# Mamba scan with B and C rows spread by DMA, half of its drives made by ScalarE, and sixteen experts loaded after it

## The reference

```python
xin, z = split(layernorm(x) @ in_proj.T)
xc  = silu(causal_conv8(xin))
dt, B, C = split(xc @ x_proj.T)              # 8, 16 and 16 columns
delta = softplus(dt @ dt_proj.T + bias)
h_t = h_(t-1) * exp(delta_t * A[:, n]) + delta_t * B_t[n] * xc_t      # for each channel and state n
y_t = sum over n of h_t * C_t[n]
out = ((y + xc * D) * silu(z)) @ out_proj.T  # then residual, norm and a 128-512-128 ReLU network
```

## Time and profile before

| | |
|---|---|
| median of 3 runs | 788.13 us (787.86 to 789.38) |
| span of the profiled execution | 791.8 us, from its first to its last instruction |
| the profiled execution's own time | not listed apart from its span; the span is 3.7 us above the median of the runs |
| busy: PE, DVE, ACT, POOL | 642.2, 529.6, 405.3, 414.8 us |
| DMA | 84.43 MB |

### The profile page before, as it was taken

How to read it: one execution, slowest core, us unless ns; L and a number is a source line. 1 busy time by engine, 2 the same in 40 slices (tenths; PEclk the granted TensorE clock), 3 DMA queues, 4 the chain that set the end, 5 groups by cost and what they waited for, 6 DMA issues and landing times.

```text
span 791.8 us, 17837 instructions
## 1 busy us (share of the span) xinstructions
PE 642.2 (81%) x4583; PEld 434.2 (55%) x4583; DVE 529.6 (67%) x1518; ACT 405.3 (51%) x880; POOL 414.8 (52%) x488
## 2 busy tenths in 40 slices
PE   4974888888865599999287799999888648999890
PEld 2311333324653499999143355555456517999890
DVE  6779999996565266555378889899645633665444
ACT  2645777772321165665075567677644303566550
POOL 5203999985667255454277534444444672545450
PEclk9965999999995799999699599999999867999995
DMA  7979999922011122221618311211002112222215
GB/s 205 321 254 256 251 247 249 249 58 80 8 34 47 53 81 70 72 72 41 185 36 287 128 51 49 59 49 35 4 0 98 34 53 58 78 71 67 67 42 166
DMA packets 88312, 84.43 MB, mean 107 GB/s; under 512 B 12897, under 2 KB 77401, under 8 KB 87977
## 3 DMA queue, kind: packets, MB, share of 16 engines
q1 hardware_dynamic: 82600, 71.89, 33.9%
q0 software_dynamic: 5632, 11.58, 4.5%
HBM read 37.98 MB, written 45.46 MB: 105 GB/s over the span
## 4 chain that ended last, share of the span: by engine, by line
PE 33%; DVE 7%; issue 5%; DMA 2%; SPq 2%; ACT 2%; POOL 1%; ACTq 0%; DVEq 0%; POOLq 0%
PE bank L643 7%; PE bank L652 6%; PE bank L2017 5%; PE bank L1948 3%; PE bank L1951 2%; DVE t_peak L1768 2%; PE bank L2127 2%; PE bank L1993 2%; PE bank L2118 1%; DVE X L249 1%; PE bank L636 1%; SPq L1427 1%; DMA work<-results 1%; PE bank L2044 1%; DVE t_tabs L1848 0%
## 5 line engine op out<-in xcount | busy, mean ns | idle before, releaser
L806 POOL TENSOR_TENSOR UN<-work 128x512 f32<-128x512 f32 x64 | 81.7, 1289 | 55.4 <-DVE work L1034 54.7
L1768 DVE TENSOR_REDUCE t_peak<-bank 128x1 f32<-128x512 f32 (+2 forms) x192 | 104.0, 592 | 9.5 <-PE bank L1951 7.4
L445 ACT ACTIVATE t_v_tiles<-bank,t_e_b1all 128x128 f32<-128x128 f32 x224 | 64.0, 368 | 63.5 <-PE bank L643 58.8
L445 ACT ACTIVATE m_dx_tiles<-bank,m_e_b1all 128x128 f32<-128x128 f32 x224 | 64.0, 369 | 60.0 <-PE bank L643 57.8
L410 POOL DMA_INDIRECT results<-t_A,t_e_to_row x56 | 53.8, 961 | 67.1 <-DVE t_A L559 33.0
L410 POOL DMA_INDIRECT results<-m_XC,m_e_to_row x56 | 53.8, 961 | 63.7 <-issue 33.9
L1181 PE MATMUL bank<-UN,ident 128*128 128x512 f32 x128 | 71.0, 637 | 14.2 <-POOL UN L806 13.6
L1034 DVE TENSOR_TENSOR_SCAN work<-bank,work 128x512 f32<-128x512 f32 x64 | 76.6, 1216 | 8.3 <-POOL UN L806 7.0
L549 DVE COPY UN<-w1all 128x512 f32 x112 | 48.2, 430 | 40.5 <-PE bank L643 28.4
L652 PE MATMUL bank<-w2all,t_v_tiles 128*128 x448 | 60.6, 279 | 2.7 <-ACT t_v_tiles L445 2.0
L643 PE MATMUL bank<-t_A,UN 128*128 128x128 f32 x448 | 61.0, 280 | 0.0
(11 more groups left out here) (323 smaller groups left out, 1441.8 us busy)
## 6 DMA issues: line engine op xcount, KB each, us to landing
xrows<-m_nothing SPq DMA_DIRECT2D x25, 1032.0 KB, 17.9
w1all<-in_e_w SPq DMA_DIRECT2D x6, 1024.0 KB, 12.2
work<-results SPq DMA_DIRECT2D x16, 256.0 KB, 4.5
m_dx_tiles<-xrows SPq DMA_DIRECT2D x56, 64.5 KB
t_v_tiles<-xrows SPq DMA_DIRECT2D x56, 64.5 KB
t_tabs<-stacks SPq DMA_DIRECT2D x32, 96.0 KB, 2.2
work<-stacks SPq DMA_DIRECT2D x32, 96.0 KB, 2.1
m_tabs<-in_e_b SPq DMA_DIRECT2D x1, 1536.0 KB
```

Source lines behind the costliest of these rows:

```text
L445: ins = act.activation(e.hid[:, mp, f * P:f * P + P], core.tiles(2 + mp)[:, f, :], ACT.Gelu, bias=row(e.b1all, x)[:, f:f + 1])
L806: g.tensor_tensor(hc[:, k % 4, :], h[:, k % 2, :], c_sb[:, k % 2, :], ALU.mult).then_inc(hc_ready, 1)
L1768: v.tensor_reduce(peak[p][:, a, ss[0]:ss[-1] + 1, qt], bank[:, f, 0:len(ss) * w].rearrange("p (j n) -> p j n", n=w), AX_X, ALU.max).then_i ...
```

## The change

1. **B and C rows.** `split`, `pick`, `spread_b`, `spread_c` and ACT's copies of C are gone. `select` is one f32 matmul for all 40 columns. ACT copies its result (`keep_sel`), and SP writes the 32 rows of B and C to HBM and reads each row back over all partitions, 256 KB a transfer: 64 for C into eight buffers and 32 for B into four. The buffers lie where the last 16 experts' weights go.
2. **Drives.** The pattern `DAGADADAGADADAGA` says who makes the drive of each of 16 steps. In 8 steps (A) ACT scales time-major tiles of `DX` by a column of B in four instructions of 128 columns, and PE turns them into a PSUM bank with four transposes. In 5 steps (D) DVE multiplies the B row, now in SBUF, by `DX`; in 3 (G) POOL does.
3. **Buffers.** `h` has four buffers instead of two. Decays have six: three in PSUM, for D and G steps, and three in SBUF, for A steps. So a scan still has one input in PSUM and one in SBUF.
4. **Step sizes.** Only batch 0's part of softplus on DVE is done ahead of the scan. Of batches 1 to 3 the four DVE instructions (of 512 columns) follow steps 2, 4, 6 and 8 of the batch before. On PE six matmuls on the identity stand ahead of the first transposes of `DX`.
5. **Experts.** Eight experts are loaded at the start and 16 after the scan. The 25.8 MB of zeros are gone: once the rows are counted, SP and ACT each write 12 blocks of 64.5 KB behind the last row of 12 experts, ahead of SP's reads and of ACT's gates, in both mixtures.

```diff
-REGION = NB * T
+REGION = NB * T + P
+KINDS = "DAGADADAGADADAGA"
+LATE_EXPERTS = 8
...
+    def clear_ends(self, eng, experts):
+        e, core = self, self.core
+        eng.wait_ge(e.end_row_ready, 1)
+        for x in experts:
+            r = eng.value_load(e.end_row[0:1, x:x + 1], min_val=0, max_val=XROWS - P)
+            eng.dma_start(core.xrows[bass.ds(r, P), :], core.nothing[:]).then_inc(core.zeroed, 16)
...
     def sync(self, sp):
         e, core = self, self.core
+        e.clear_ends(sp, range(0, NE, 2))
+        sp.wait_ge(core.zeroed, 16 + 16 * NE * e.layer)
         sp.wait_ge(core.sent, 16 * TOPK * NT * e.layer)
...
     def scalar(self, act):
         e, core = self, self.core
+        e.clear_ends(act, range(1, NE, 2))
         act.wait_ge(e.gdiff_ready, 1)
...
+            def keep_rows(b):
+                sp.wait_ge(sel_copied, b + 1)
+                sp.dma_start(bc_rows[b], sel[b % 2][0:2 * NS, :]).then_inc(rows_kept, 16)
+                sp.wait_ge(rows_kept, 16 * b + 16)
+            def stream(k):
+                b, n, i = k // NS, k % NS, before(B_STEPS, k)
+                if kind(k) != "A":
+                    if i >= 4:
+                        sp.wait_ge(h_ready, LEAD + B_STEPS[i - 4] + 1)
+                    sp.dma_start(b_sb[:, i % 4, :], bc_rows[b, n].partition_broadcast(P)).then_inc(core.back_in[i % 4], 16)
+                if k >= AHEAD:
+                    sp.wait_ge(hc_ready, LEAD + k - AHEAD + 1)
+                sp.dma_start(c_sb[:, k % AHEAD, :], bc_rows[b, NS + n].partition_broadcast(P)).then_inc(core.slot_in[k % AHEAD], 16)
...
             for k in range(NB * NS):
-                if on_pool(k + 2):
-                    g.wait_ge(b_copied, pool_drives(k + 3))
-                    g.tensor_tensor(dbx[3], dbx[3], DX[:, (k + 2) // NS, :],
-                                    ALU.mult).then_inc(pool_dbx_ready, 1)
+                if k + 2 in G_STEPS:
+                    drive(k + 2)
...
+            keep_sel(NB - 2)
+            time_step(NB - 2)
             convolved(NB - 1)
             act.preload_act_table(ACT.Exp)
+            keep_sel(NB - 1)
             act.wait_ge(alog_in, 16)
             act.activation(a_neg[:], a_neg[:], ACT.Exp).then_inc(a_exp, 1)
+            act.wait_ge(abs_ready, LEAD + NB - 1)
+            act.activation(EXPV[:, 0:NB - 1, :], EXPV[:, 0:NB - 1, :], ACT.Exp, scale=-1.0).then_inc(exp_ready, 1)
+            time_step(NB - 1)
...
+            decay(0)
+            keep_dxT(0)
+            scale_drive(1, range(TT))
+            for k in range(0, NB * NS, 2):
+                if k:
+                    decay(k)
+                if k % NS == NS - 4 and k // NS < NB - 1:
+                    keep_dxT(k // NS + 1)
+                if k + 3 < NB * NS:
+                    scale_drive(k + 3, early)
+                decay(k + 1)
+                if k + 3 < NB * NS:
+                    scale_drive(k + 3, late)
...
             def drive(k):
-                v.wait_ge(b_ready, LEAD + k + 1)
-                v.wait_ge(h_ready, LEAD + k - 3)
-                v.tensor_tensor(dbx[k % 4], bank[:, 4 + k % 2, :], DX[:, k // NS, :], ALU.mult).then_inc(dbx_ready, 1)
+                i = before(B_STEPS, k)
...
+                v.tensor_tensor(dbx[:, i % 4, :], b_sb[:, i % 4, :], DX[:, k // NS, :], ALU.mult).then_inc(dbx_ready, 1)
...
-                if k < NB * NS - 1 and not on_pool(k + 1):
+                if k + 1 in D_STEPS:
                     drive(k + 1)
                 scan(k)
+                b, n = k // NS, k % NS
+                if b < NB - 1 and n in (2, 4, 6, 8):
+                    delta(b + 1, n // 2 - 1)
...
+            keep_busy(pe, core, 5, 6)
...
+            turn_dx(0)
+            skip(0)
+            for k in range(NB * NS):
+                if k + 1 in A_STEPS:
+                    turn_drive(k + 1)
+                if k % NS == NS - 6 and k // NS < NB - 1:
+                    turn_dx(k // NS + 1)
+                if k >= 1:
...
+                    add_state(k - 1)
```

More of the change, by code:

```diff
@@ L243, in combine @@
     tiles = range(b * TT, b * TT + TT)
-    v.wait_ge(core.back_in[b], 16 * TOPK * layer)
+    v.wait_ge(core.back_in[b], 16 * B_FILLS + 16 * TOPK * layer)
     for k in range(TOPK):
@@ L690, in mamba @@
     DELTA = st.sb("DELTA", [P, NB, T])
-    BC = batches(bc_xT[0:96, :].bitcast(BF16))
+    sel = [bc_xT[0:ROWS, p * T:p * T + T] for p in range(2)]
+    bc_rows = nc.dram_tensor("bc_rows", (NB, 2 * NS, T), F32).ap()
     work = core.work
@@ L697, in mamba, with decay_of @@
     hc = core.UN[:].rearrange("p (b t) d -> p b (t d)", t=TT)
[L698 to L703, removed]
+    late_w1 = core.w1all[:, LATE_EXPERTS:, :]
+    late_w2 = core.w2all[:].rearrange("p e k n -> p e (k n)")[:, LATE_EXPERTS:, :]
+    c_sb, dbx = late_w1[:, 0:8, :], late_w1[:, 8:12, :]
+    b_sb, scaled, dxT, decay_sb = (late_w2[:, x:y, :] for x, y in ((0, 4), (4, 7), (7, 9), (9, 12)))
+    h = tabs[:, 0:4 * T].rearrange("p (i n) -> p i n", n=T)
+    kind = lambda k: KINDS[k % NS]
+    before = lambda steps, k: sum(j < k for j in steps)
+    DECAY, A_BANK = (2, 3, 6), (4, 5)
+    def decay_of(k):
+        steps = A_STEPS if k in A_STEPS else B_STEPS
+        i = steps.index(k)
+        return decay_sb[:, i % 3, :] if k in A_STEPS else bank[:, DECAY[i % 3], :], steps[i - 3] if i >= 3 else None
     YZ = DX
@@ new lines, in keep_dxT, with scale_drive @@
+            def keep_dxT(b):
+                act.wait_ge(dxt_turned, b + 1)
+                act.activation(dxT[:, b % 2, :], bank[:, 7, :], ACT.Identity).then_inc(dxt_ready, 1)
+            def scale_drive(k, tiles):
+                b, n, a = k // NS, k % NS, before(A_STEPS, k)
+                if 0 in tiles:
+                    act.wait_ge(dxt_ready, b + 1)
+                    act.wait_ge(adrive_ready, LEAD + a - 2)
+                for t in tiles:
+                    ins = act.activation(scaled[:, a % 3, t * P:t * P + P], dxT[:, b % 2, t * P:t * P + P], ACT.Identity,
+                                         scale=b_turned[:, b, t, n:n + 1])
+                if TT - 1 in tiles:
+                    ins.then_inc(scaled_ready, 1)
@@ new lines, in decay, with first_norm @@
+            def decay(k):
+                b, n = k // NS, k % NS
+                act.wait_ge(dx_ready, b + 1)
+                out, previous = decay_of(k)
+                if previous is not None:
+                    act.wait_ge(h_ready, LEAD + previous + 1)
+                act.activation(out, DELTA[:, b, :], ACT.Exp, scale=a_neg[:, n:n + 1]).then_inc(decay_ready, 1)
+            def first_norm(i):
+                if i % TT == 0:
+                    act.wait_ge(ln_x.shift_ready, i // TT + 1)
+                act.activation(X1[:, i, :], X[:, i, :], ACT.Identity, bias=ln_x.shift[:, i:i + 1],
+                               scale=ln_x.rs[:, i:i + 1]).then_inc(ln_x.normed, 1)
@@ new lines, in _ @@
+            early, late = range(TT // 2), range(TT // 2, TT)
+            decay(0)
[11 more added lines that the diff above has]
+                    scale_drive(k + 3, late)
+                if k // NS == 1 and k % 4 == 0:
+                    first_norm((NB - 1) * TT + k % NS // 4)
@@ L1150, in _ @@
                 time_step(b - 2)
+                turn_b(b - 2)
                 convolve(b)
-            select(NB - 2)
-            time_step(NB - 2)
-            select(NB - 1)
-            time_step(NB - 1)
-            pe.wait_ge(pick_ready, 1)
-            pe.wait_ge(bc_split, LEAD + NB)
+            for b in range(NB - 2, NB):
+                select(b)
+                time_step(b)
+                turn_b(b)
+            keep_busy(pe, core, 5, 6)
             pe.wait_ge(relu_ready, LEAD + NB)
```

264 lines of the change are left out of this document (142 added, 122 removed).

## The result

The changed kernel takes 798.13 us (median of 5 runs, 790.44 to 798.57) where the kernel before takes 787.86 (of five runs; the 788.13 of the table above is of three): a ratio of 1.0129, 95% interval 1.0101 to 1.0156, so about 10 us slower. The prediction was 788.8, with a range up to 797.

The account below looks back on a forecast made before the run. The scan was taken as DVE's, POOL close behind, then a chain of norms and sends. Terms -5.8 (ahead of the scan), +6.5 (scan) and 0 gave +0.7 on the median: 788.8 us, range 780.5 to 797.

Parts of the forecast that it names:

- Clearing: Before the expert stages' reads: clearing transfers issued by 259 to 263, landed about 2 us later, hidden; 0 to +2, taken 0.
- Rival 4: Expert seams: clearing ends late because loaded-address transfers cost ACT 1.5 us or more; +2.5 a layer, 793; chance 0.06.
- In the scan: Scan 1 to scan 63: 114.9 us against 108.4, +6.5, with bounds of -0.9 and +14.6.
- exclusion: In the scan: two-SBUF-input DVE instructions and POOL's exclude each other; the one behind pays all but some 0.13 us of its length.
- the walk: One scan batch stepped through in order with assumed durations, scan 1.17 apart, POOL 1.26: next batch's first scan at 29.9 us.
- The same walk without exclusion: In the scan: a batch takes 27.85 us if DVE and POOL do not block each other; scan 107.5, -0.9.
- Drives of DVE with a mean near 1.0: In the scan, a sign that the forecast holds: DVE's drives average near 1.0 us in place of 0.67.
- PE's order: In the scan: PE turns drive k+1 after add_state(k-2), so S(k+1) starts 1.8 us after POOL ends product k-2; two places.
- Ahead of the scan: Before the scan: scan 0 at 60 instead of 70.05, scan 1 at 66 against 71.76; -5.8, between -8.5 and -3.2.
- Zeros, experts, stream: Omitted zeros, late expert weights and the 96 transfers of 256 KB in the scan: each costs or gains 0.
- The PE clock as a rival: Before and in the scan: idle gaps lower PE's clock, `convolve(3)` +3.7, each fall in the scan 1 to 2; 792 to 797; chance 0.22.
- PE runs at the low clock inside the scan: In the scan: one of the listed signs that would show the prediction wrong; no size of its own.

Follow-up runs that it names:

- ends_wide: The changed kernel with the same rows cleared in 16 pieces of 4128 bytes a transfer instead of 128 of 516: 798.6 us, ratio 1.0154 to before.
- the first profile: The profiled execution of the changed kernel as first measured, 790.44 us (span 788.9), where its median is 798.13 us.
- the second: The profile of a repeat of the changed kernel with no edit; the repeat measured 797.8 us, ratio 1.0123 to before.
- ends_only: The kernel before, without its zeros and with the changed kernel's clearing behind each expert's last row: 791.9 us against 786.2, ratio 1.0061.
- drive_psum: The changed kernel with DVE's drives reading delta times x from a PSUM bank, copied there by PE once a batch: 786.8 us, ratio 1.0000 to before.
- turn_early: The changed kernel with PE turning the drive of step k+2, not k+1, ahead of the state sum of step k-1: 789.7 us, ratio 1.0049 to before.
- fill_gaps: The changed kernel with one extra identity matmul in each of PE's two 1.8 us gaps before the time steps of batches 0 and 1: 795.9 us, ratio 1.0116.
- both: The changed kernel with drive_psum and turn_early together, nothing else: 782.5 us against 785.5, ratio 0.9975 to before.
- combined: The changed kernel with both, fill_gaps, GpSimd clearing behind the last eight experts, first drive from SBUF, 8 identity passes instead of 12: 776.3 us, ratio 0.9863.

## Why the prediction was wrong

**Clearing: the step that failed.** "Hidden by 0 to 3 us; at the upper bound 1 us late, in each of two layers: 0 to +2, I take 0." Its price for an issue was right (12.46/12 = 1.04 us on ACT, 13.44/12 = 1.12 on SP, from 249.3 instead of 247.2, done at 262.8). Wrong was what follows, "about 2 us later landed": the last clearing landed 5.2 us behind its issue (262.5 to 267.8), 6.1 in the other layer. And what it never asked was what 24 transfers of 64.5 KB do to the last twelve sends, which go through the same DMA engines in the same 14 us. It compared when the clearing lands with when the sends land, priced the first as if the engines were free, and took the second from the trace of before. PE saw the last send 4.2 us behind its end instead of 1.5. The two landed within 0.2 to 0.4 us of each other in each profile that has all 24 between the sends (but ends_wide), so the reads had to wait for both; the seams grew by 2.4 and 3.2 us in the first profile and by 2.6 and 3.3 in the second, and ends_only alone costs 4.8. Rival 4 had the right sign and nearly the price (+2.5 a layer) with the wrong mechanism, an issue of 1.5 us or more, and so got 0.06.

The Trainium skill (DMA: Bandwidth & Descriptors, Queues, rings and completion order) says that each DMA engine takes turns between its queues, and that the write that counts up a semaphore lands only after every earlier write of that engine, whatever queue it came from. By that rule a send's signal waits for clearing writes that are ahead of it on its engine. The lag of 4.2 us with 24 transfers between the sends and of 1.6 with 16 of them agrees, and so do the last send and the last clearing that land together; which of the two parts of the rule does it, no run here separates.

**In the scan: mechanism right, size low.** "+6.5" came out +10.3 and +10.1 (118.7 and 118.5 us against 108.4), inside the bounds of -0.9 and +14.6. A middle batch was walked at 29.9 and took 30.8 (scan 16 at 92.89 to scan 48 at 154.46); the first fifteen steps took 29.3 and 28.2, not 28.0, the last batch 27.8, not 26.9. The delays from exclusion were sized well: 3.9 us a batch over five drives in the walk, 5 x (1.37 - 0.67) = 3.5 measured. Too small was the rest. POOL's products took 1.44 in the mean where the walk had 1.26, three of the four delta instructions 0.9 to 1.7 where 0.61 was taken (the fourth 0.67), and PE's turns came late at more than two places a batch: ten waits, 7.5 us, from 72 to 176, of which 3.1 at two places with PE at the low clock. ACT's scaling, taken at 0.31 us a piece, took 0.39; it cost nothing that shows, since ACT itself waited 14.0 us for PE's turns. How the 3.6 us divide among these was not separated. (The walk's own sum is off by 0.2: two batches of 29.9 are 59.8, not 60.0.) "The same walk without exclusion gives 27.85" a batch, 107.5 in all; drive_psum, which takes the drives out of it, measured 27.9 and 107.7. "Drives of DVE with a mean near 1.0" was contradicted by the walk's own delays, which give 1.45; 1.37 was measured.

**Both causes were in the walk, and neither was acted on.** It named exclusion and PE's order as the two sources of loss. turn_early and drive_psum, each a few lines, give 8 and 11 us of scan.

**Ahead of the scan: right.** Scan 1 was given as 66, between 63.3 and 68.6, and came at 63.6 and 65.9, and 65.5 to 66.2 in the four others whose order there is almost the same. Scan 0 was given as 60 and came at 59.2 and 62.0. The first profile is the case of a clock that holds until 48 us, the others that of a fall before.

**Zeros, experts, stream: right at 0.** ends_only shows it for the zeros. The late weights moved in 180 to 222 us, and in the scan no engine stood waiting for a row of B or C; 256 KB landed in 3.7 to 3.8 us.

**The PE clock as a rival: present, small.** PE ran at the low clock for stretches of the scan (granted 0.90 to 0.91 in four of its 20 us windows, where before had 1.00), but fill_gaps, with 1.00 from 80 to 180 us, still took 116.3. So I estimate the clock at about 2 of the scan's 10 us, from one profile of fill_gaps; its waits for turns come to 4.3 us from 72 to 176, where the first profile, with two of them at the low clock, has 7.5. "PE runs at the low clock inside the scan" was one of the prediction's own signs of being wrong, and it came about in this small measure.

**The sum.** With the measured terms, -5.8 + 10.1 + 5.9 = +10.2 against the +0.7 of the prediction: 5.9 of the error is the clearing, 3.6 the scan. The range missed by 1.1 us because it held the clearing at 2 and no case in it had the clearing late and the scan above its middle together.

**What stays open.** Of the 3.7 us by which the profiled execution of before stood above its median, most is in the last stage: 133.8 us from the first tile of the second expert stage to the end, 129.7 to 131.5 in all eleven other profiles. Single executions of one kernel differ by up to 8 us, and I did not settle what sets which one gets which. For both and combined the places give 6 and 3 us more gain against before than the ratios do.

## What to carry to other kernels

A transfer that is moved among others has two prices: when it lands itself, and how much later those land that it travels with; check the DMA share of that window, not only the time at which its own wait ends. An elementwise instruction that gets a second SBUF input beside a busy GpSimd should be given a PSUM operand if a bank can be found: one identity matmul a batch bought back 11 us here. And when a walk names an in-order queue that holds an urgent instruction behind one that waits, try the other order before anything else.

## What the runs showed of the hardware

- A DVE instruction with two SBUF inputs can be held for longer than one POOL instruction: in combined a delta instruction of 0.67 us (L1112) took 3.07 us at 118.32, beside POOL products that went on at 1.25 each, and 1.84 at 90.94.
- Clearing 128 rows of 516 bytes at a loaded address, in HBM, went at 156 GB/s together with the sends, with the DMA engines full; with 4128-byte pieces from 16 partitions at 129.
- GpSimd issued eight such transfers in 4.34 us, 0.54 each, where ACT and SP took 1.04 and 1.12. This is not like for like: GpSimd had loaded the addresses between its sends (253.9 to 262.6), and on ACT and SP the issue alone took 0.34.
